# A gated feed-forward block on Trainium2: the order of GpSimd's divisions, the engine of the token pairs, and the place of a bias

## The reference

```python
x = x + (softmax(q @ k.T * scale) @ v) @ w_proj + b_proj
def fp4_quant_dequant(x):                 # blocks of 16 values
    scale = maximum(max(abs(xb)) / 6, 1e-12)
    q = GRID[searchsorted(MID, abs(xb / scale))] * sign(xb) * scale
gate, up = fp4(xn) @ fp4(w_gate).T, fp4(xn) @ fp4(w_up).T      # xn = layernorm(x), 256 -> 704
x = x + fp4(silu(gate) * up) @ fp4(w_down).T                   # 704 -> 256
```

## Time and profile before

| | us |
|---|---|
| three runs | 1421.0, 1421.72, 1427.67 (median 1421.72) |
| the profiled execution, its own time | 1429.85 |
| its span, first to last instruction | 1427.6 |
| busy: PE, DVE, ACT, POOL | 1265.9, 964.3, 760.1, 672.8 |
| mean granted TensorE clock | 0.921 of full speed |
| gated block | 1315.1 to the end |

### The profile page before, as it was taken

The page is one execution under the profiler, slowest core; times in us unless marked ns, Lnnn a source line. Parts: engine busy times, 40 slices in busy tenths (PEclk is TensorE's granted clock), DMA queues, the critical chain, the costliest instruction groups (busy, mean ns, idle before and its releaser), DMA issues. The chain is left out here.

```text
span 1427.6 us, 34694 instructions
## 1 busy us (share of the span) xinstructions
PE 1265.9 (89%) x12166; PEld 1058.4 (74%) x12166; DVE 964.3 (68%) x1987; ACT 760.1 (53%) x1371; POOL 672.8 (47%) x602
## 2 busy tenths in 40 slices
PE   5799999999999688459996899999999997766787
PEld 3688888888887467358874788888888886555455
DVE  5577777777777565456406677777777776565995
ACT  2577777777776211012143677777777775123111
POOL 2556656656654223044232566566566653324341
PEclk9999999999999885569998899999999999868998
DMA  6677776776774220625537577767767762100000
GB/s 198 175 203 188 182 195 177 184 203 177 186 171 103 47 48 3 208 63 182 181 111 227 165 192 181 194 177 186 200 178 185 199 149 66 35 1 3 0 12 19
DMA packets 106724, 198.31 MB, mean 139 GB/s; under 512 B 43662, under 2 KB 63791, under 8 KB 106641
## 3 DMA queue, kind: packets, MB, share of 16 engines
q1 hardware_dynamic: 105104, 193.32, 51.3%
q0 software_dynamic: 1536, 3.88, 0.9%
HBM read 88.26 MB, written 10.62 MB: 69 GB/s over the span
## 5 line engine op out<-in xcount | busy, mean ns | idle before, releaser
L844 POOL TENSOR_SCALAR cross_prob<-cross_prob,cross_inverse 128x1024 f32<-128x1024 f32 x256 | 288.7, 1128 | 348.3 <-DVE cross_inverse L593 348.3
L771 ACT ACTIVATE cross_prob<-cross_negated,cross_negmax 128x1024 f32<-128x1024 f32 x256 | 294.9, 1152 | 148.7 <-DVE cross_negmax L585 148.4
L585 DVE CUSTOM_DVE_ANT_0 cross_negated<-cross_scores,cross_bias 128x1024 f32<-128x1024 f32 x256 | 313.6, 1225 | 31.1 <-PE cross_scores L476 13.7
L489 PE MATMUL cross_turn<-ident,cross_prob 128*128 128x128 f32 x2048 | 270.9, 275 | 14.9 <-POOL cross_prob L844 11.8
L489 PEld LDWEIGHTS cross_turn<-ident,cross_prob 128*128 128x128 f32 x2048 | 240.9, 142 | 54.7 <-POOL cross_prob L844 15.8
L780 ACT COPY cross_probT<-cross_turn 128x512 f32<-128x512 f32 x256 | 149.6, 584 | 68.7 <-PE cross_turn L489 67.6
L476 PE MATMUL cross_scores<-cross_keys,cross_qbd 96*128 96x512 f32 x512 | 169.9, 414 | 12.6 <-POOL cross_qbd L836 12.6
L601 DVE COPY cross_probT<-cross_turn 128x512 f32<-128x512 f32 x256 | 175.6, 686 | 5.5 <-PE cross_turn L489 5.5
L824 POOL TENSOR_TENSOR cross_ctx_lo<-cross_raw,cross_ctx_hi 128x512 fp32r<-128x512 f32 x120 | 156.0, 1302 | 24.6 <-ACT cross_ctx_hi L747 24.6
L419 PE MATMUL cross_out<-cross_wv_hi,cross_ctx_lo 128*128 128x256 f32 x488 | 147.9, 303 | 0.0
L421 PE MATMUL cross_out<-cross_wv_hi,cross_ctx_hi 128*128 128x256 f32 x488 | 137.7, 282 | 0.0
(11 more groups left out here) (269 smaller groups left out, 2061.4 us busy)
## 6 DMA issues: line engine op xcount, KB each, us to landing
cross_keys<-cross_key_hi SPq DMA_DIRECT2D x512, 128.0 KB, 2.3
cross_raw<-in_ctxT SPq DMA_DIRECT2D x32, 1024.0 KB, 5.6
cross_keys<-cross_key_lo SPq DMA_DIRECT2D x256, 128.0 KB, 2.4
cross_bias<-bias_rows SPq DMA_DIRECT2D x32, 512.0 KB, 3.6
up_sb<-in_moe_w SPq DMA_DIRECT2D x8, 1024.0 KB, 9.8
down_sb<-in_moe_w SPq DMA_DIRECT2D x8, 1024.0 KB, 11.6
cross_stacked_q<-q_rows SPq DMA_DIRECT2D x90, 64.0 KB, 2.0
q_rows<-cross_negated SPq DMA_DIRECT2D x8, 256.0 KB, 2.4
```

The costliest lines, as they stand in the source:

```text
L489: last = pe.transpose(ps_t[part][:, k * P:(k + 1) * P], prob[n % 2][:, kt * P:(kt + 1) * P], ident)
L585: dve.tensor_tensor_reduce(negated[n % 2], ps_s[n % 2][:, :], bias_sb[par][:, :], -1.0, 3.0e38, ALU.add, ALU.min, negmax[:, n % 2:n % 2 + ...
L771: act.activation(prob[n % 2][:, :], negated[n % 2], ACT.Exp, bias=negmax[:, n % 2:n % 2 + 1], scale=-1.0, accum_out=total[:, n % 2:n % 2 + ...
L844: pool.tensor_scalar(prob[n % 2][:, :], prob[n % 2][:, :], inverse[:, n % 2:n % 2 + 1], 1.0, ALU.mult, ALU.mult).then_inc(prob_ready, 1)
```

## The change

Three things. In the gated block GpSimd's divide(i) now waits on a new semaphore `powered`, raised when VectorE has made the powers of tile i-1; `round` is split into `powers` and the rest for it. A token pair is quantized wholly by VectorE (`quantize_pair`), and VectorE's order is: pair 2, multiply(0), joins 4 to 7, multiply(1), round(0), pair 3, multiply(2), round(1), multiply(3), round(2), add(0), pair 4, and so on. GpSimd's order is the four roots, divide(0), and then divide(i), finish(i-1). The projection's bias is added to `x` by GpSimd in the rotary block before, behind the two memsets, and the joins wait for PE alone.

```diff
--- before.py
+++ after.py
@@ -917,7 +917,7 @@
                 take_moments(dve, i, x, stats, moments, added, seen)
             take_moments(dve, NT, x, stats, moments, added, seen)
             dve.wait_ge(seen, 2 * NT)
-def rope_block(nc, tag, xnT, wqkv, b_row, cos, sin, halves, ident, qkT, value, zero=None):
+def rope_block(nc, tag, xnT, wqkv, b_row, cos, sin, halves, ident, qkT, value, zero=None, residual=None):
 
 
 
@@ -947,6 +947,10 @@
             if b_row is None:
                 for parity in range(2):
                     pool.memset(value[parity][:, :, :], 0.0).then_inc(cleared, 1)
+            if residual is not None:
+                x, row = residual
+                for i in range(NT):
+                    pool.tensor_tensor(x[:, i, :], x[:, i, :], row, ALU.add)
 
         @block.tensor
         def _(pe):
@@ -1670,11 +1674,15 @@
         n = n or self.width
         return eng.tensor_tensor(self.by_block(self.v[:, 0:n]), self.by_block(x), self.wide(self.inverse, slice(0, n // HD)), ALU.mult)
 
+    def powers(self, dve, c, power, n=None):
+        n = n or self.width
+        v, power = self.v[:, 0:n], power[:, 0:n]
+        c.link(dve.tensor_scalar(power.bitcast(U32), v.bitcast(U32), self.EXPONENT, None, ALU.bitwise_and))
+        return dve.tensor_scalar(power, power, 1.0, self.LAST_PLACE, ALU.max, ALU.mult)
+
     def round(self, dve, c, power, total, n=None):
         n = n or self.width
         v, power, total = self.v[:, 0:n], power[:, 0:n], total[:, 0:n]
-        c.link(dve.tensor_scalar(power.bitcast(U32), v.bitcast(U32), self.EXPONENT, None, ALU.bitwise_and))
-        c.link(dve.tensor_scalar(power, power, 1.0, self.LAST_PLACE, ALU.max, ALU.mult))
         c.link(dve.tensor_tensor(total, v, power, ALU.add))
         return dve.tensor_tensor(v, total, power, ALU.subtract)
 
@@ -1683,7 +1691,9 @@
         return eng.tensor_tensor(self.by_block(out), self.by_block(self.v[:, 0:n]), self.wide(self.scale, slice(0, n // HD)), ALU.mult)
 
 
-def gated_block(nc, tag, aT, w, b_row, x, moments, gate_upT, downT, ident, out):
+def gated_block(nc, tag, aT, w, x, moments, gate_upT, downT, ident, out):
+
+
 
 
 
@@ -1708,13 +1718,12 @@
         ps_u = [psum(f"u{i}", [P, HW]) for i in range(2)]
         ps_t, ps_y, ps_x = psum("t", [P, 8, P]), psum("y", [P, D]), psum("x", [P, G, 2 * P])
         ps_p = [ps_t[:, 4 * i:4 * i + 2, :].rearrange("p c q -> p (c q)") for i in range(2)]
-        biased, projected, joined, seen = sem("biased"), sem("projected"), sem("joined"), sem("seen")
+        projected, joined, seen = sem("projected"), sem("joined"), sem("seen")
         stat_step, rooted = sem("stat_step"), sem("rooted")
-        tokens_scaled, tokens_divided, tokens_rounded = sem("tokens_scaled"), sem("tokens_divided"), sem("tokens_rounded")
-        tokens_quantized_v, tokens_quantized_p = sem("tokens_quantized_v"), sem("tokens_quantized_p")
-        tokens_turned, tokens_copied = sem("tokens_turned"), sem("tokens_copied")
+        tokens_quantized, tokens_turned, tokens_copied = (sem(f"tokens_{n}") for n in ("quantized", "turned", "copied"))
         gate_ready, up_ready, silu_done, gated = sem("gate_ready"), sem("up_ready"), sem("silu_done"), sem("gated")
         scaled, divided, rounded, quantized = sem("scaled"), sem("divided"), sem("rounded"), sem("quantized")
+        powered = sem("powered")
         last_quantized = sem("last_quantized")
         step, turned, turn_copied = sem("step"), sem("turned"), sem("turn_copied")
         down_ready, added, stored = sem("down_ready"), sem("added"), sem("stored")
@@ -1733,10 +1742,7 @@
 
             def turn_tokens(k):
                 a, b = groups[k]
-                if k < 2:
-                    pe.wait_ge(tokens_quantized_v, k + 1)
-                else:
-                    pe.wait_ge(tokens_quantized_p, k - 1)
+                pe.wait_ge(tokens_quantized, k + 1)
                 if k:
                     pe.wait_ge(tokens_copied, k)
                 for g in range(G):
@@ -1843,7 +1849,6 @@
 
             def join(i):
                 dve.wait_ge(projected, i + 1)
-                dve.wait_ge(biased, i + 1)
                 dve.tensor_tensor(x[:, i, :], x[:, i, :], ps_p[i % 2], ALU.add).then_inc(joined, 1)
                 dve.wait_ge(joined, i + 1)
                 dve.bn_stats(stats[:, i, :], x[:, i, :]).then_inc(seen, 1)
@@ -1864,24 +1869,19 @@
                 part = xn[:, i, :]
                 c.link(tq.scales(dve, c, part, D))
                 c.link(tq.divide(dve, part, D))
+                c.link(tq.powers(dve, c, tpower, D))
                 c.link(tq.round(dve, c, tpower, ttotal, D))
-                tq.multiply(dve, part, D).then_inc(tokens_quantized_v, 1)
-
-            def token_scales(k):
+                tq.multiply(dve, part, D).then_inc(tokens_quantized, 1)
+
+            def quantize_pair(k):
                 c.wait()
-                if k == 2:
-                    dve.wait_ge(tokens_quantized_v, 2)
-                else:
-                    dve.wait_ge(tokens_quantized_p, k - 2)
-                tq.scales(dve, c, flat(xn[:, groups[k][0]:groups[k][1], :])).then_inc(tokens_scaled, 1)
-
-            def token_round(k):
-                dve.wait_ge(tokens_divided, k - 1)
-                if k == 2:
-                    dve.wait_ge(tokens_quantized_v, 2)
-                else:
-                    dve.wait_ge(tokens_rounded, k - 2)
-                tq.round(dve, c, tpower, ttotal).then_inc(tokens_rounded, 1)
+                dve.wait_ge(tokens_quantized, k)
+                part = flat(xn[:, groups[k][0]:groups[k][1], :])
+                c.link(tq.scales(dve, c, part))
+                c.link(tq.divide(dve, part))
+                c.link(tq.powers(dve, c, tpower))
+                c.link(tq.round(dve, c, tpower, ttotal))
+                tq.multiply(dve, part).then_inc(tokens_quantized, 1)
 
             def multiply(i):
                 for h in range(2):
@@ -1900,6 +1900,8 @@
                 dve.wait_ge(divided, i + 1)
                 if i:
                     dve.wait_ge(rounded, i)
+                q[i % 2].powers(dve, c, power).then_inc(powered, 1)
+                dve.wait_ge(powered, i + 1)
                 q[i % 2].round(dve, c, power, total).then_inc(rounded, 1)
 
             def add(i):
@@ -1914,37 +1916,32 @@
             normalize(0)
             quantize_tile(0)
             normalize(1)
-            dve.wait_ge(tokens_quantized_v, 1)
+            dve.wait_ge(tokens_quantized, 1)
             quantize_tile(1)
             normalize(2)
             normalize(3)
-            token_scales(2)
+            quantize_pair(2)
             multiply(0)
-            token_round(2)
-            join(4)
-            join(5)
-            shift(2)
+            for pair in range(2, 4):
+                join(2 * pair)
+                join(2 * pair + 1)
+                shift(pair)
             multiply(1)
             round_hidden(0)
-            join(6)
-            join(7)
-            shift(3)
             normalize(4)
             normalize(5)
-            token_scales(3)
+            quantize_pair(3)
             multiply(2)
             round_hidden(1)
-            token_round(3)
             multiply(3)
             round_hidden(2)
             add(0)
             normalize(6)
             normalize(7)
-            token_scales(4)
+            quantize_pair(4)
             multiply(4)
             round_hidden(3)
             add(1)
-            token_round(4)
             for i in range(5, NT):
                 multiply(i)
                 round_hidden(i - 1)
@@ -1957,54 +1954,25 @@
 
         @block.gpsimd
         def _(pool):
-            def bias(i):
-                pool.tensor_tensor(x[:, i, :], x[:, i, :], b_row, ALU.add).then_inc(biased, 1)
-
             def root(pair):
                 at = slice(2 * pair, 2 * pair + 2)
                 pool.wait_ge(stat_step, pair + 2)
                 pool.tensor_tensor(rstd[:, at], shifted[:, at], power_[:, at], ALU.pow).then_inc(rooted, 1)
 
-            def token_divide(k):
-                pool.wait_ge(tokens_scaled, k - 1)
-                tq.divide(pool, flat(xn[:, groups[k][0]:groups[k][1], :])).then_inc(tokens_divided, 1)
-
-            def token_multiply(k):
-                pool.wait_ge(tokens_rounded, k - 1)
-                tq.multiply(pool, flat(xn[:, groups[k][0]:groups[k][1], :])).then_inc(tokens_quantized_p, 1)
-
             def divide(i):
                 pool.wait_ge(scaled, i + 1)
+                if i:
+                    pool.wait_ge(powered, i)
                 q[i % 2].divide(pool, hidden[i % HIDDEN][:, :]).then_inc(divided, 1)
 
             def finish(i):
                 pool.wait_ge(rounded, i + 1)
                 q[i % 2].multiply(pool, hidden[i % HIDDEN][:, :]).then_inc(quantized, 1)
 
-            for i in range(4):
-                bias(i)
-            root(0)
-            root(1)
-            for i in range(4, NT):
-                bias(i)
```

(25 more changed lines are left out.)

## The result

The changed kernel took 1431.31 us (median of 20 runs, 1427.1 to 1437.82), the one before 1424.93 (median of 20, 1421.0 to 1430.56). The ratio is 1.0042, with an interval of 1.0029 to 1.0054: 6.0 us slower, 4.1 to 7.7 (the two medians lie 6.4 apart). The forecast was 5.9 slower; its absolute figure, 1427.6, stood on the median of three runs, 3.2 us under that of twenty. The profiled execution has a span of 1434.0 us.

The account below looks back on a forecast made before the run. PE, almost full with VectorE close behind, was taken to bound the gated block's main stretch, which starts at finish(1). 4.6 us there plus 1.3 in the rotary block made +5.9: 1427.6 us, range 1420.5 to 1432.5.

Parts of the forecast that it names:

- Step 1: Gated block's rounds: the new semaphore only moves the stall from the second power operation to `v`, 0.0 us per tile.
- Rival B: Rounds and rotary block: two-input VectorE operations run free beside GpSimd's divide, no slowdown, 1422.4 us; chance 0.15.
- The bias leaving: Gated block: tile 0's token quantization no longer lies beside GpSimd's bias adds, so everything behind comes 1.40 us earlier.
- The bias in the rotary block: Rotary block: GpSimd's adds hold about three two-input VectorE operations, delaying PE by 1.3 us, between 0 and 2.0.
- Finish(1): Gated block: VectorE's new order puts more work ahead, so GpSimd's finish(1), and turn(1) with it, comes 4.1 us later.
- After finish(1): PE's full stretch: finish(3) ready 0.8 us late, turn(4)'s old 0.34 stall gone, +0.5 us up to down(5).
- The tail "the same": Gated block's end: after add(4) and down(5), the tail keeps its length.
- rival C: Gated block's tail: the clock holds, so down(5) and down(6) give back 5.1 us, 1422.5 us; chance 0.15.
- Rival D: Gated block: PE's new gaps of about 4 us make the clock fall more often, +9, 1430.7 us; chance 0.25.

Follow-up runs that it names:

- experiment 2: Kernel before with only the bias moved: into the rotary block, ratio 0.9984; or into the self attention, 0.9965.
- experiment 3: Changed kernel with the bias moved to the self attention: ratio 1.0013 to the kernel before; its pair is the kernel before with that bias place, 0.9965.
- experiment 4: Changed kernel with token pairs 3 and 4 behind the rounds, 1.0022; kernel before with VectorE dividing and multiplying the pairs at their old place, 1.0021.
- experiments 4 and 6: Here: kernel before with pairs divided and multiplied on VectorE, 1.0021; kernel before with bias in attention and round(6) ahead of multiply(7), 0.9951.
- early last round: Kernel before with the bias in the self attention and tile 6 rounded ahead of multiply(7): ratio 0.9951, median 1418.86 us.

## Why the prediction was right

- **Step 1, the reorder, 0.0.** Shown: `v` 1.96 us (1.9), second power 0.53, divide 2.03 (2.1), and the block unchanged to 0.01 us with and without the semaphore. The experts block's rows had priced an operation that the gated block never showed beside GpSimd. The gated block had a nearer case, used only to price the bias: tile 0's token division, two-input as well, took 0.90 us beside GpSimd's adds (at 1322.47), tile 1's 0.43. Rival B falls with it.
- **The bias leaving, -1.40:** -1.45 (P to G, 12.23 to 10.78). At down(5) 0.67 of it is left in experiment 2, because the first gate_up ran longer at the low clock; a tail 3.98 us shorter, which no step foresaw, came on top.
- **The bias in the rotary block, +1.3:** the first tile +1.47, and PE's turn waits 1.79 us instead of 0.33, +1.46. It then runs on as forecast but for 0.2 us (21.67 us to the last turn, 21.46 before), of which the second tile, whose first multiply is held 0.50, makes 0.16. Together 1.67, inside the stated bound of 2.0; the 3.18 of experiment 2 is outside it, since the forecast took for granted that nearly three adds are over before VectorE comes. (Three holds of 0.40 make 1.2, not 1.3.)
- **Finish(1), +4.1:** from the first gate_up, which comes 1.40 sooner in the forecast, that is +5.5. Turn(1) came 5.25 later there, and 5.44 in the pair of experiment 3. The normalizes took 1.79 us for two, where two alone take 0.73: 1.06 of wait for the 1.1 foreseen. Multiply(1)'s scale took 0.35 instead of 0.19.
- **After finish(1), +0.5:** 0.74 in the pair of experiment 3. It is made as foreseen: from turn(1) to turn(3), which waits for finish(3), 21.17 us instead of 19.89, so +1.28 where 0.8 was taken (the scales' wait of 0.41 for finish(1) is the rest), and -0.54 from there to down(5), where turn(4)'s 0.34 went. Between the changed kernel and the one before it is 2.40: the same +1.28, and then down(2) ran 4.64 instead of 2.95. That PE's wait itself is 2.88 us, and not 1.28, comes from turn(1) and down(0), which ran in 0.87 and 2.95 instead of 1.39 and 4.16: PE merely arrives sooner at the same finish(3).
- **The tail "the same":** 1.24 us shorter in these two executions (17.01 against 18.25), with add(4)'s gap unchanged at 3.38. That is rival C's mechanism in small; it didn't hold, down(6) ran 5.31.
- **Rival D** happened in part: gate_up(3) ran slow after its wait of 3.89 (2.71 us in the quarter shown, where a quarter at full clock takes 1.35 to 1.45). That cost nothing, as PE still waited 0.99 us for finish(1) behind it. Down(2) ran slow after 2.88 and cost 1.7. The first four projections, 6.60 us against 3.73, added 2.3 us in this execution that no step foresaw; the same code ran them in 3.73 in experiment 3. In absolute time the median, 1431.31, is nearer to this rival's 1430.7 than to the forecast's 1427.6, but 3.2 us of that is the base of three runs.

By the profiled executions' own terms: order and engine +6.2, bias out -1.45, rotary block +1.67 or +3.18, together +6.4 to +7.9, against +6.0 (4.1 to 7.7) measured. By the ratios: -5.0 for the bias in the attention, +6.8 for order and engine on top, +4.1 for the bias's move on to the rotary block, together 5.9, and each step is known to 3 or 4 us only. So the mechanism was right, and order and engine are the slowdown; that 5.9 met 6.0 to a tenth is luck, because the clock moved single terms by 1 to 4 us. Of the +6.2, the pairs' early place costs 2.7, and 3.5 is left for VectorE's doing them and the joins' new place, which no run separates; alone in the old order the engine costs 4.7.

## What to carry to other kernels

Here the stall between two engines that hold each other moved with the semaphore and didn't go: look for what the order puts beside the long operation next, and price it from wherever the trace shows the same meeting, even in another block. Work moved off an engine that looks idle is paid on the one whose end the next stage waits for; ask what is queued behind it there. An add that nobody waits for belongs beside operations that read PSUM, where these eight cost nothing, not beside two-input ones, where they cost 1.67 to 3.18 us. And a part whose price hangs on how two queues happen to meet should be read in executions at both clocks.

## What was not expected of the hardware

- A 0.69 us memset by GpSimd that starts beside a running two-input operation isn't held (0.69 us), where a divide is (2.03 us for 1.39).
- The hold is the same both ways: VectorE's and GpSimd's held operations alike ended their own length less 0.14 us behind the releaser's end (experiment 4).
- Whichever of the power operations meets GpSimd is held: in kernels of experiments 4 and 6 it was the first (a uint32 mask), held to 1.49 and 1.60 us, like the second one in the earlier trace rows.
- The granted clock's falls differ between executions and edits by more than most terms here. Down(5), after a wait of 3.38 or 3.39 us, took 4.44 to 5.76 us in all nine executions that have that wait, for the 2.95 of 2.4 GHz. Elsewhere the wait ahead doesn't tell: in experiment 3 turn(1) came after 2.18 us and turn(3) after 2.87, and both and the downs behind them ran at 2.4 GHz; in the changed kernel turn(3) came after the same 2.88 and the down(2) behind it took 4.64; down(6) of the early last round took 4.66 after a wait of 1.54.
